# An audio tower: the experts' first-layer weights kept in memory and copied per tile by VectorE

## The reference, cut to what matters

```
p      = softmax(x @ w_gating)                 # 6 experts
e, g   = argmax(p), p1 / (p1 + p2 + 1e-9)      # p1, p2: the two largest shares
hidden = gelu(layernorm(x) * gamma @ w1[e])    # 128 -> 512
out    = out + g * (hidden @ w2[e])            # 512 -> 128
```

## Time and profile before

| | |
|---|---|
| median of three runs | 797.01 us (795.95 to 797.87) |
| profiled execution | 796.16 us |
| its span | 794.3 us |
| mean granted TensorE clock | 0.875 |
| TensorE busy | 600.7 us, 76% |
| VectorE busy | 634.3 us, 80% |
| ScalarE busy | 525.4 us, 66% |
| GpSimd busy | 281.5 us, 35% |
| transfers | 56.52 MB, mean 71 GB/s |
| weight loads of the experts' first layer | 28 of 256.0 KB |

### The profile page before, as it was taken

The page is one execution under the profiler, slowest core; times in us unless marked ns, Lnnn a source line. Parts: engine busy times, 40 slices in busy tenths (PEclk is TensorE's granted clock), DMA queues, the critical chain, the costliest instruction groups (busy, mean ns, idle before and its releaser), DMA issues.

```text
span 794.3 us, 10840 instructions
## 1 busy us (share of the span) xinstructions
PE 600.7 (76%) x3096; PEld 467.8 (59%) x3097; DVE 634.3 (80%) x1298; ACT 525.4 (66%) x849; POOL 281.5 (35%) x311
## 2 busy tenths in 40 slices
PE   6997652818264463719977799897899999999997
PEld 3564552818264462718555579864666766666665
DVE  1687397999999999999788752357899989988953
ACT  1488999899999999897224344362677576565542
POOL 0465100010000000000038754444477667665632
PEclk9998877869596867768968699997999999999999
DMA  5372031445555544444151266511000000000000
GB/s 188 116 265 89 1 61 35 84 78 103 96 98 95 102 76 89 76 76 76 59 177 31 69 179 191 170 44 34 1 0 11 1 11 11 1 9 10 1 11 19
DMA packets 26381, 56.52 MB, mean 71 GB/s; under 512 B 4199, under 2 KB 15568, under 8 KB 25856
## 3 DMA queue, kind: packets, MB, share of 16 engines
q0 software_dynamic: 5728, 24.56, 16.4%
q1 hardware_dynamic: 19288, 30.52, 12.5%
q10 hardware_dynamic: 1320, 0.90, 0.4%
HBM read 29.91 MB, written 10.17 MB: 50 GB/s over the span
## 4 chain that ended last, share of the span: by engine, by line
PE 34%; DVE 34%; issue 15%; ACT 10%; POOL 2%; DMA 2%; SPq 1%; DVEq 0%; ACTq 0%; POOLq 0%
DVE s_R L1352 5%; DVE s_R L1339 4%; PE psum L1930 4%; DVE s_R L1363 3%; PE psum L2210 3%; DVE s_R L1848 3%; PE psum L2147 2%; PE psum L2139 2%; PE psum L2197 2%; DVE s_R L1344 2%; PE psum L2243 2%; DMA s_R<-x_sorted 2%; DVE s_R L1695 2%; PE psum L2199 1%; PE psum L2198 1%
## 5 line engine op out<-in xcount | busy, mean ns | idle before, releaser
L2002 PE MATMUL psum<-s_xn_lo,s_split_hi 128*128 128x368 f32 x256 | 95.0, 371 | 137.7 <-ACT s_R L957 134.8
L2002 PEld LDWEIGHTS psum<-s_xn_lo,s_split_hi 128*128 128x128 f32 x256 | 54.7, 214 | 142.5 <-ACT s_R L957 137.5
L716 POOL DMA_DIRECT2D s_xnfm<-s_R x14 | 16.9, 1206 | 257.4 <-DVE s_R L1363 257.4
L1358 DVE TENSOR_TENSOR_SCAN s_R<-s_R 128x2944 f32<-128x2944 f32 x16 | 100.7, 6292 | 0.8
L2003 PE MATMUL psum<-s_xn_hi,s_split_lo 128*128 128x368 f32 x256 | 92.1, 360 | 0.0
L2004 PE MATMUL psum<-s_xn_hi,s_split_hi 128*128 128x368 f32 x256 | 91.5, 357 | 0.0
L1119 ACT ACTIVATE s_xnfm<-psum,s_cols 128x368 f32<-128x368 f32 x96 | 49.4, 564 | 54.0 <-PE psum L2199 53.9
L2210 PE MATMUL psum<-s_xnfm,s_R 128*128 128x368 f32 x192 | 66.1, 479 | 0.7 <-DVE s_R L1718 0.7
L964 ACT ACTIVATE s_R<-psum,s_cols 128x736 f32<-128x736 f32 x64 | 56.1, 876 | 13.8 <-PE psum L2004 10.1
L1339 DVE SCALAR_TENSOR_TENSOR s_R<-s_R 128x2944 f32<-128x2944 f32 x16 | 51.4, 3213 | 10.2 <-ACT s_R L922 6.4
L775 POOL TENSOR_TENSOR s_R<-s_R 128x368 f32<-128x368 f32 x47 | 45.6, 971 | 38.3 <-DVE s_R L1718 18.4
(11 more groups left out here) (272 smaller groups left out, 1613.2 us busy)
## 6 DMA issues: line engine op xcount, KB each, us to landing
s_xnfm<-s_R POOLq DMA_DIRECT2D x14, 1472.0 KB, 10.5
s_R<-in_w SPq DMA_DIRECT2D x28, 256.0 KB
s_R<-in_xg SPq DMA_DIRECT2D x7, 744.0 KB, 4.2
x_sorted<-in_x_init SPq DMA_DIRECT2D x1, 5082.0 KB
s_wBC<-in_wBC SPq DMA_DIRECT2D x8, 256.0 KB, 2.8
s_R<-in_v SPq DMA_DIRECT2D x2, 1024.0 KB
s_R<-x_sorted SPq DMA_DIRECT2D x28, 66.0 KB
s_R<-in_w SPq DMA_DIRECT2D x1, 1536.0 KB, 6.8
```

The source lines that it names most:

```text
L1358: dve.tensor_tensor_scan(bufB[:, u], ra[:, u], bufB[:, u], 0.0, ALU.mult, ALU.add).then_inc(ra_free, 1)
L2002: pe.matmul(bank(c), w_hi[:, s, u, k, :], xn_lo[:, a:b], start=True, stop=False)
```

## The change

The first layers of all six experts are loaded at once, after the state-space layer, ahead of `w2`. For each tile VectorE reads the expert's number into a register and copies that expert's 128x512 weights from `w1` into one of two slots (`w1_slot`), one tile ahead; TensorE's layer 1 reads the slot. SyncE's 28 loads per tile and their four semaphores are gone. `w1` and the slots take 2048 columns more than the four slots before, and the attention's `qkv` moves from behind the experts' tiles to the last columns of `XN`, whose rows have been scattered by then.

```diff
-        w1 = take(NSL, HID)
+        w1 = take(NE, HID)
+        w1_slot = take(2, HID)
         w2 = take(NE, HT, D)
         XN = take(B, XD, parts=LS)
+        xn_end = taken[0]
...
-        w1_ready = [sem("w1_ready%d" % s) for s in range(NSL)]
+        w1_ready, w1_filled = sem("w1_ready"), sem("w1_filled")
...
-        taken[0] = d_end
+        taken[0] = qkv_at = xn_end - 6 * CT
         qkv = take(2, 3, CT)
...
             sp.wait_ge(skip_mm, NH)
+            sp.dma_start(w1, t["w1"]).then_inc(w1_ready, 16)
             sp.dma_start(w2, t["w2"]).then_inc(w2_ready, 16)
...
-            def load_w1(t_, s, first=False):
-                sp.reg_load(w_at[s], tile_e[0:1, bass.ds(t_, 1)])
-                if not first:
-                    sp.wait_ge(h_mm, t_ - 1)
-                sp.dma_start(w1[:, s], t["w1"][:, bass.ds(sp.snap(w_at[s], min_val=0, max_val=NE - 1), 1)]
-                             .rearrange("p a h -> p (a h)")).then_inc(w1_ready[s], 16)
...
                 for s in range(NSL):
                     load_rows(i * NSL + 2 + s, s % 2)
-                    load_w1(i * NSL + 4 + s, s)
...
+            e_at = dve.alloc_register("e_at")
+
+            def fill_w1(t, u):
+                if not (isinstance(t, int) and t >= NTILE):
+                    dve.reg_load(e_at, tile_e[0:1, bass.ds(t, 1)])
+                    if not (isinstance(t, int) and t < 2):
+                        dve.wait_ge(h_mm, t + 1)
+                    dve.tensor_copy(w1_slot[:, u], w1[:, bass.ds(dve.snap(e_at, min_val=0, max_val=NE - 1), 1), :]
+                                    .rearrange("p a h -> p (a h)")).then_inc(w1_filled, 1)
...
                 if i == NP - 1:
                     full_tiles()
+                    dve.wait_ge(w1_ready, 16)
+                    dve.wait_ge(tile_ready, 2)
+                    fill_w1(0, 0)
                 choose(i)
...
             other_tiles()
+            dve.wait_ge(tile_ready, 4)
...
                 dve.wait_ge(h_mm, t + 1)
                 dve.tensor_scalar(xeT[:, u], psum[:, u, 0:TS], col("ffn_gamma"), None, ALU.mult).then_inc(xeT_ready, 1)
+                fill_w1(t + 1, 1 - u)
...
             def layer1(t, s):
                 u = s % 2
-                pe.wait_ge(w1_ready[s], (t - s) * 4 + 16)
+                pe.wait_ge(w1_filled, t + 1)
...
-                    ins = pe.matmul(psum[:, 2 + u, j * TS:(j + 1) * TS], w1[:, s, j * D:(j + 1) * D], xeT[:, u],
+                    ins = pe.matmul(psum[:, 2 + u, j * TS:(j + 1) * TS], w1_slot[:, u, j * D:(j + 1) * D], xeT[:, u],
```

More of the change, by code:

```diff
@@ L457, in audio_tower @@
         assert d_end <= W_AT and taken[0] == W_AT + W_COLS
-        taken[0] = d_end
+        taken[0] = qkv_at = xn_end - 6 * CT
         qkv = take(2, 3, CT)
-        assert taken[0] <= W_AT
         taken[0] = hid_end
@@ L509, in audio_tower @@
         assert taken[0] <= W_AT
-        assert taken[0] <= ot_at
+        assert taken[0] <= qkv_at
         nF = Norm("f", 1)
@@ L599, in _ @@
             x_at = [sp.alloc_register("x_at0"), sp.alloc_register("x_at1")]
-            w_at = [sp.alloc_register("w_at%d" % s) for s in range(NSL)]
             def load_rows(t_, u):
@@ L609, in rows_from @@
                     .then_inc(xt_ready[u], 16)
-            def load_w1(t_, s, first=False):
-                sp.reg_load(w_at[s], tile_e[0:1, bass.ds(t_, 1)])
-                if not first:
-                    sp.wait_ge(h_mm, t_ - 1)
-                sp.dma_start(w1[:, s], t["w1"][:, bass.ds(sp.snap(w_at[s], min_val=0, max_val=NE - 1), 1)]
-                             .rearrange("p a h -> p (a h)")).then_inc(w1_ready[s], 16)
-            for s in range(2):
-                load_w1(s, s, True)
             for u in range(2):
@@ L624, in _ @@
                 rows_from(u, u)
-            for s in range(2, NSL):
-                load_w1(s, s, True)
             with sp.Fori(0, NFULL // NSL - 1) as i:
@@ L643, in _ @@
                 load_rows(NTILE - NSL - 2 + s, s % 2)
-                load_w1(NTILE - NSL + s, s)
             for u in range(2):
```

## The result

The changed kernel takes 791.16 us (median of six runs, 788.75 to 792.65), the kernel before 796.48 over six runs: a ratio of 0.9934, 95% interval 0.9916 to 0.9952. The forecast was 791.3. The profiled execution took 791.74 us, with a span of 789.9 against 794.3.

The account below looks back on a forecast made before the run. Rows late behind weight loads in SyncE's full queue bound the expert stage: 797.01 + 0.7 (first fill) - 3.4 (pace) - 1.7 (hole) - 1.7 (clock) + 0.4 (last tiles) = 791.3 us; range 787.5 to 797.5.

Parts of the forecast that it names:

- What bounds the stage: Expert stage: row loads come late behind 256 KB weight loads in SyncE's full queue, and TensorE idles for rows.
- Rival C: Expert stage: scatters and memory slow the rows, not weights; pace stays 2.11 us a tile, 798.1 us; chance 0.12.
- The pace of the tiles: Tiles 0 to 23: without weight loads 1.93 us a tile, 44.4 us plus 0.7 against 48.5: -3.4 us.
- the gate steps: VectorE's gate_shares and gate_ratio beside fills, between tiles 1 and 3: +0.35 us each, +0.7 together.
- The fill: VectorE, each tile: register load 0.3 us and weight copy 0.41, free under TensorE's 1.93 us in plain tiles.
- Rival D: VectorE becomes the bound: each fill waits for GpSimd's running scatter, 1.7 us a fill, 806 us; chance 0.10.
- The first fill: Before the last choose, ahead of tile 0: register load and copy with nothing beside them, +0.7 us (0.3 to 1.2).
- the clock's fall behind tile 24: Behind the hole at tile 24: with a shorter hole the granted clock stays up, -1.7 us.
- The hole at tile 24: Tile 23's transpose to tile 24's first layer: results land 4.5 us after request, 3.8 us instead of 5.51, -1.7.
- rival A: Tile 24: the wait moves to expert results, still 6.3 us; hole and clock unchanged, 794.7 us; chance 0.22.
- The last tiles: Last four tiles: fills join early_rows, statistics and normalisation on VectorE, +0.4 us beside the clock's -1.7.
- The sum: Whole kernel: all terms together -5.7 us, from 797.01 to 791.3 us; chance 0.42.

Follow-up runs that it names:

- e1: Kernel before, but weight loads from tile 4 on bring 16 of 512 columns, with all issues kept: 788.85 us, ratio 0.9919.
- e2: Kernel before, but ScalarE instead of SyncE issues the weight loads from tile 4 on, all bytes kept: 796.46 us, ratio 1.0014.
- e9: Changed kernel with 239 KB per tile loaded again by SyncE from tile 4 on, into regions nobody reads: 796.48 us, ratio 1.0006.
- e3: Changed kernel with a second VectorE copy of 448 columns in every tile but the first: 792.23 us, ratio 0.9964 to the kernel before.
- e4: Changed kernel with the first tile's fill moved behind the list of the other tiles: 788.11 us, ratio 0.9915 to the kernel before.
- e5: Changed kernel with the first tile's fill between the last place and the other tiles' list: 788.38 us, ratio 0.9906 to the kernel before.
- e11: e5 run again, beside e10 on one chip: 789.80 us, ratio 0.9925 to the kernel before.
- e10: The changed kernel run again with a second profile, beside e11 on one chip: 789.61 us, ratio 0.9920 to the kernel before.
- e7: e6 with the fill for tile 25 behind the first group's statistics instead of ahead: 788.16 us, ratio 0.9905 to the kernel before.
- e6: e5 with ScalarE requesting the first group's results one tile earlier: 789.57 us, ratio 0.9922 to the kernel before.

## Why the prediction was right, step by step

*What bounds the stage.* Right, and shown three ways: without the bytes nearly all rows are in time though the queue is as full as before (e1), with the bytes they are late though the queue is free (e2), and putting them back takes the whole gain away (e9). One half of the reason given weighs little: "its queue is full" describes SyncE rightly, but e1 kept it full and had the gain all the same, less 1 to 2 us. The 9.1% of SyncE in the chain of the earlier trace rows was for the most part time on the way to a late transfer, not its cause. Rival C is refuted by the same three.

*The pace of the tiles.* Forecast 44.4 us and 0.7 for the gate steps, measured 45.49. The gate steps cost 0.76 (2.37 and 2.25 us for tiles 2 and 3, where a plain tile takes 1.93). Plain tiles take 1.96 us on average, not 1.93; the second profile has 1.94 (and 45.05 us for tiles 0 to 23), and e1, without any fills, 1.97. So the difference is not the fills'.

*The fill.* Copy 0.43 us (forecast 0.41, from the scaling L1344 and the subtraction L1632), register load 0.307 at the median (forecast 0.3). In plain tiles it is free or nearly so, and e3 shows that another 0.4 us would be, too. Rival D was that a copy waits for GpSimd's running scatter. In the changed kernel's profile 21 of 28 copies begin while a scatter runs, one of them 0.10 us into it (460.29, scatter from 460.19 to 461.11), and the longest copy takes 0.48 us. e3's copies fall otherwise, and those that begin 0.53 to 0.59 us into a scatter take 0.18 to 0.19 us longer than beside none (448 columns alone: 0.38 us; the scatter beside this one began at 504.59):

```profile
505.17 0.57 DVE L1558 COPY s_R<-s_R 128x448 f32<-128x448 f32 x1
```

The Trainium skill, SBUF — State Buffer, section "Who interferes with whom", has one of the two block for the other's whole instruction. Here the measurement decides: a copy lost up to 0.05 us in the changed kernel and up to 0.19 in e3, never a whole scatter, and the median scatter kept its 0.96 us. So a part of rival D's mechanism is there, at a small part of the 0.98 us that D put on every fill.

*The first fill.* The term that was mis-sized: +0.7 forecast, +1.75 measured, outside its range of 0.3 to 1.2. Two parts. VectorE's queue starts the register load only behind its last small operation and needs 0.76 us from there to the copy. The load takes 0.56 of it, not the median's 0.31, and arithmetic on the register 0.09, which the forecast left out (the chain of waits of the changed kernel, 448.5 to 450 us):

```profile
448.85 0.56 DVEq L1553
...
449.44 0.09 DVEq L1556
```

The price was taken from the median (0.305) of TensorE's loads. The first of them is the 0.496 that the earlier trace rows give as the longest, and all others took 0.312 or less, so the row that bore on a first load was there. With the copy this part is +1.07. And TensorE's wait for VectorE grows from 2.14 to 3.23 us. The granted clock falls to 0.50, its lower level, during this wait in both kernels; before, it comes back between 457 and 458 us, ahead of the filler's end at 458.29, and in the changed kernel it stays at 0.50 from 450 to 460, so that the filler takes 5.25 us: +0.7. Where the fill is moved (e4, e5, e11) both go. The prediction treated the clock's fall behind tile 24 and did not reckon with a longer wait elsewhere.

*The hole at tile 24.* Results landed 4.65 us behind their request (502.29 to 506.94; forecast 4.5, before 6.34), so rival A did not happen (in e5 they took 5.20, and tile 24's first layer came 4.45 us behind tile 23's transpose, so this term is not steady); the hole shrank by 1.56 (forecast 1.7) and the clock stayed up.

*The last tiles.* -0.98 us against -1.3: if the clock gave the 1.7 of its windows, the fills cost 0.7 and not 0.4. TensorE's transposes for the attention wait 0.37 us for VectorE's normalisation in the changed kernel (0.20 in e10) and 0.95 in e3; e7 did not show a gain in time for moving one fill.

*The sum.* -5.7 forecast, -3.8 found in the stage's profile (-4.3 in the second), -5.3 in the medians (-6.4 in the second set). Parts of the kernel that were not changed differ between executions by up to 2 us. So the mechanism of the forecast is shown and its size is not confirmed to the microsecond: that the median fell within 0.2 us of 791.3 is luck.

## What to carry to other kernels

When small transfers on the chain share their engines with large ones, take bytes away before issues: a full issue queue cost 1 to 2 us here (an estimate from e1), 256 KB per tile nearly all. A copy between memory tiles on an engine that is idle for 60% of the stage (VectorE was busy for 25.92 of 66.1 us) is a cheap price for that; but place its first instance, with its register load, in an existing wait, and look at how long the clock stays low behind a longer wait of TensorE. And a step shown in a profile can stay invisible in medians; compare stretch by stretch before claiming it.

## What the hardware showed that was not expected

- The clock falls to its lower level during TensorE's wait for VectorE in every profile; behind a wait longer by some 1.1 us it came back later. In four profiles (the changed kernel twice, e3, e9) TensorE waits 3.19 to 3.31 us and runs the whole filler at 0.50, in 5.25 us; in the kernel before and in e1, e2, e4, e5, e6, e7 and e11 it waits 2.10 to 2.23 us, the clock is back before the filler ends, and it takes 4.41 to 4.55. Why it comes back when it does, no run here isolates.
- Half the filler left the clock low into the first four tiles (2.05 us for 8 matmuls instead of 1.13) and cost 4.6 us for the 2.4 it saved.
- The first register load of the expert's number took 0.55 to 0.65 us on VectorE (0.56 in the changed kernel, 0.65 in e5, 0.55 in e4) against a median of 0.31, and made most of the 0.76 us from the last small operation to the first copy; in plain tiles 0.22 to 0.34 us of idle time remain ahead of the copy.
- VectorE's copy and GpSimd's scatter hinder each other only in a part of the scatter. Over ten profiles, copies that begin up to 0.49 us into a scatter, or from 0.77 us on, take what they take alone (0.38 to 0.43 us). Those that begin between 0.53 and 0.75 us are longer, by up to 0.19 us, the more so the earlier they begin.
